# One core, an image filter beside a text encoder: inputs loaded in another order, VectorE's first step in an order of its own, smaller masks, and the residual added inside a feed-forward sum

## The reference

```
h = filter(x)                                  # 8 images of 256 x 256
h = concat([h, text(x_txt)], axis=1)           # 8 sequences of 128 tokens, D = 256
h = h + windowed_attention(layernorm(h))
h = h + spiking_ffn(layernorm(h))              # relu, square, project, count of spikes

filter:  u = sigmoid(2 o);  q = 0
         10 times: q = max(q - 0.5*(d_rows(u)*vf1 + d_cols(u)*vf0), 0)
                   Tq = div_rows(vf1*q) + div_cols(vf0*q);  u = sigmoid(2*(o - Tq))
text:    h = emb[x_txt] + positions
         4 layers: h = ln(h + attention(h));  h = ln(h + relu(h@w1 + b1)@w2 + b2)
```

## Time and profile before

| | |
|---|---|
| time, three runs | median 1001.82 us (1001.42 to 1001.96) |
| the profiled execution's own time | 999.17 us |
| its span, first to last instruction | 997.3 us |
| mean granted TensorE clock | 0.976 |
| busy in the span | PE 905.2, DVE 834.9, ACT 699.3, POOL 122.3 us |

### The profile page before, as it was taken

One profiled execution on the slowest core, in us unless ns is written; L12 is line 12 of the kernel. 1 busy time (PEld: TensorE's weight loads), 2 busy tenths in 40 slices (PEclk: granted clock), 3 DMA queues, 4 the chain that ended last, 5 costly groups with the idle time before them and its releaser, 6 DMA issues.

```text
span 997.3 us, 18874 instructions
## 1 busy us (share of the span) xinstructions
PE 905.2 (91%) x6960; PEld 700.2 (70%) x6960; DVE 834.9 (84%) x1160; ACT 699.3 (70%) x2252; POOL 122.3 (12%) x147
## 2 busy tenths in 40 slices
PE   5489999999999999999999997889998999999997
PEld 4267777777777777777777775767675766667675
DVE  2999999999999999999999998987899599352443
ACT  2666876976877877877876875757767686767842
POOL 6201011011011011101101111101010111000000
PEclk9699999999999999999999999999998999999999
DMA  7311120031010121010220010000001000100000
GB/s 173 113 35 28 66 89 19 22 122 45 18 45 17 32 90 39 17 46 14 70 80 11 17 38 11 12 22 12 27 17 38 17 22 17 44 27 2 17 1 32
DMA packets 24925, 39.00 MB, mean 39 GB/s; under 512 B 4001, under 2 KB 20609, under 8 KB 23553
## 3 DMA queue, kind: packets, MB, share of 16 engines
q1 hardware_dynamic: 24448, 36.74, 11.6%
q0 software_dynamic: 384, 1.05, 0.5%
HBM read 22.21 MB, written 5.24 MB: 28 GB/s over the span
## 4 chain that ended last, share of the span: by engine, by line
DVE 47%; PE 25%; ACT 16%; issue 9%; DMA 2%; POOL 1%; SPq 0%; DVEq 0%; POOLq 0%; ACTq 0%
ACT prob L1086 7%; PE ps_t L849 7%; DVE f L1726 4%; DVE f L1753 4%; PE ps_m L860 4%; DVE f L1748 4%; DVE p L1738 4%; DVE f L1757 4%; DVE neg_max L1762 4%; DVE f L1743 3%; ACT u L1073 3%; DVE f L1721 2%; DVE f L1710 2%; PE ps_s L796 2%; DVE f L1699 2%
## 5 line engine op out<-in xcount | busy, mean ns | idle before, releaser
L1086 ACT ACTIVATE prob<-ps_s,neg_max 128x128 f32<-128x128 f32 x512 | 181.3, 408 | 7.3 <-DVE neg_max L1762 7.3
L1086 ACT ACTIVATION_READ_ACCUMULATOR prob<-ps_s,neg_max 128x1 f32 x512 | 126.6, 249 | 0.0
L655 PE MATMUL ps_t<-w,hidT 128*128 128x256 f32 x512 | 125.7, 383 | 0.0
L1094 ACT ACTIVATE probT<-ps_t 128x512 f32<-128x512 f32 x128 | 81.1, 634 | 44.3 <-PE ps_t L601 28.7
L655 PEld LDWEIGHTS ps_t<-w,hidT 128*128 128x128 f32 x512 | 91.1, 190 | 12.1 <-ACT hidT L1168 3.0
L849 PE MATMUL ps_t<-km,w_fc 128*128 128x384 f32 x256 | 93.9, 503 | 1.0 <-ACT km L1282 1.0
L601 PE MATMUL ps_t<-ident,prob 128*128 128x128 f32 x512 | 81.5, 283 | 12.9 <-ACT prob L1086 6.7
L601 PEld LDWEIGHTS ps_t<-ident,prob 128*128 128x128 f32 x512 | 60.0, 144 | 36.6 <-issue 14.7
L1762 DVE TENSOR_REDUCE neg_max<-ps_s 128x8 f32<-128x1024 f32 x64 | 77.5, 1211 | 4.6 <-PE ps_s L591 4.6
L1341 ACT ACTIVATE prob<-ps_s,neg_max 128x128 f32<-128x128 f32 x192 | 53.8, 376 | 22.6 <-DVE neg_max L1935 22.2
L849 PEld LDWEIGHTS ps_t<-km,w_fc 128*128 128x128 f32 x256 | 47.5, 195 | 26.8 <-issue 3.7
(11 more groups left out here) (179 smaller groups left out, 2038.9 us busy)
## 6 DMA issues: line engine op xcount, KB each, us to landing
w<-in_w SPq DMA_DIRECT2D x8, 1024.0 KB, 5.0
u<-u SPq DMA_DIRECT2D x80, 63.0 KB
p<-p SPq DMA_DIRECT2D x80, 63.0 KB
w_attn<-in_w_attn SPq DMA_DIRECT2D x4, 768.0 KB, 5.4
out<-w SPq DMA_DIRECT2D x7, 384.0 KB, 2.5
o_all<-in_o SPq DMA_DIRECT2D x4, 512.0 KB, 3.7
filtered<-f_out SPq DMA_DIRECT2D x4, 512.0 KB, 3.2
x<-filtered SPq DMA_DIRECT2D x8, 256.0 KB, 2.8
```

The source lines that it names most:

```text
L655: last = mm(ps_t[:, 0, D * t:D * t + D], hidT[:, m, P * t:P * t + P], w2[:, m], start=False, stop=(m == MC - 1), skip_group_check=True)
L1086: last = A(prob[:, n % 2, hh], ps_s[n % 2][:, hh], ACT.Exp, scale=-1.0, bias=neg_max[:, n % 2, hh:hh + 1], accum_out=den)
L1094: A(probT[:, 4 * half:4 * half + 4].rearrange("p h k -> p (h k)"), ps_t[:, 1], ACT.Copy).then_inc(s["act_pT"], 1)
```

## The change

Five things are altered.

1. SyncE issues the first images right behind the tokens, then taps, positions, the four parts of the field (the two for the columns first, with a semaphore of their own each way) and the projection weights last. GpSimd waits for these weights before it issues gathers three to eight.
2. TensorE, VectorE and SyncE start on the first eight constants. The head mask gets its own semaphore, the row masks move behind iteration 0.
3. VectorE's `first_step` has an order of its own: iteration 0's steps before the first `head_max`, and others moved (below).
4. The window masks are 128 x 128, built four times smaller, and read four times over by a stride of zero (PE L788, ACT L1347).
5. The feed-forward bank is opened by the first product with `w2`, which now waits for the third part of the hidden layer, and `carry_ffn` stands later: in a block behind `turn_probs(a, 2, 0)`, in `fuse_first` behind `tile_turn(0, 2, 1)`.

```diff
         @block.sync
             sp.dma_start(tokens[:], d["tokens"]).then_inc(s["l_tok"], 16)
+            load_images(0).then_inc(s["l_img"], 16)
             sp.dma_start(taps[:, 0:18], ...)
             sp.dma_start(taps[:, 18:36], ...)
             sp.dma_start(pe[:], d["pe"]).then_inc(s["l_pe"], 16)
-            load_images(0).then_inc(s["l_img"], 16)
+            for comp, loaded in ((1, "l_vf"), (0, "l_vf_rows")):
+                for img in range(2):
+                    sp.dma_start(vf[64 * img:64 * img + 64, comp], ...).then_inc(s[loaded], 16)
             sp.dma_start(w_attn[:, :, 0:3 * D], ...).then_inc(s["l_qkv"], 16)
-            for img in range(2):
-                for comp in range(2):
-                    sp.dma_start(vf[64 * img:64 * img + 64, comp], ...).then_inc(s["l_vf"], 16)
...
-            sp.wait_ge(s["c_pool"], N_CONST)
+            sp.wait_ge(s["c_pool"], N_EARLY)
             rows_below(0)
...
                 if b == 1:
                     const(pool.memset(v[:], 0.0))
+                    pool.wait_ge(s["l_qkv"], 16)
...
-            def carry(bank, src):
+            def carry(bank, src, first):
-                        mm(..., ident[:], start=(t + c == 0), stop=False, ...)
+                        mm(..., ident[:], start=(first and t + c == 0), stop=False, ...)
             def carry_ffn(k):
                 pe_.wait_ge(s["pool_hr"], k + 1)
-                pe_.wait_ge(s["act_ff1"], 4 * k + 3)
-                carry(ps_t[:, 0], hT_r)
+                carry(ps_t[:, 0], hT_r, False)
...
             def ff2(k, parts):
-                        pe_.wait_ge(s["act_ff1"], 4 * k + part + 1)
+                        pe_.wait_ge(s["act_ff1"], 4 * k + max(part + 1, 3))
-                        last = mm(ps_t[...], hidT[...], w2[:, m], start=False, ...)
+                        last = mm(ps_t[...], hidT[...], w2[:, m], start=(part == 0 and m == 0), ...)
...
-                    m = mask[:, 1].rearrange("p a k -> p (a k)")
+                    m = mask[:, 1].unsqueeze(1).to_broadcast([P, 4, P])
...
             def first_step():                      # VectorE
+                head_pairs()
                 columns_apart(0)
                 columns_weighed(0)
-                head_max(0, 0)
+                positions_first()
                 rows_apart(0)
...
```

More of the change, by code:

```diff
@@ L88, in build @@
         ones = sb("ones", [P, 4 * P])
-        mask = sb("mask", [P, 2, 4, P], BF16)
+        mask = sb("mask", [P, 2, P], BF16)
         head_mask = sb("head_mask", [P, 2])
@@ L546, in carry @@
                         at = D * t + P * c
-                        mm(bank[:, at:at + P], src[:, c, P * t:P * t + P], ident[:], start=(t + c == 0), stop=False, skip_group_check=True)
+                        mm(bank[:, at:at + P], src[:, c, P * t:P * t + P], ident[:], start=(first and t + c == 0), stop=False, skip_group_check=True)
             def carry_attn(k):
@@ L652, in ff2 @@
                     if t == 0:
-                        pe_.wait_ge(s["act_ff1"], 4 * k + part + 1)
+                        pe_.wait_ge(s["act_ff1"], 4 * k + max(part + 1, 3))
                     for m in range(2 * (part % 4), 2 * (part % 4) + 2):
-                        last = mm(ps_t[:, 0, D * t:D * t + D], hidT[:, m, P * t:P * t + P], w2[:, m], start=False, stop=(m == MC - 1), skip_group_check=True)
+                        last = mm(ps_t[:, 0, D * t:D * t + D], hidT[:, m, P * t:P * t + P], w2[:, m], start=(part == 0 and m == 0), stop=(m == MC - 1), skip_group_check=True)
                 if part == 7:
@@ L687, in block_step @@
                 turn_probs(a, 2, 0)
+                carry_ffn(f)
                 ff2(f, range(2, 6))
@@ L1139, in keys_out @@
             def keys_out(k, g):
+                if k == 0:
+                    act.wait_ge(s["c_heads"], 1)
                 act.wait_ge(s[f"pe_k{g}"], k + 1)
@@ L1346, in tile_mask @@
                 for hb in range(2):
-                    last = A(quad[hb], mask[:, 0].rearrange("p a k -> p (a k)"), ACT.Copy)
+                    last = A(quad[hb].rearrange("p (a k) -> p a k", a=4), mask[:, 0].unsqueeze(1).to_broadcast([P, 4, P]), ACT.Copy)
                 last.then_inc(s["f_mask"], 1)
@@ L1669, in _, with head_pairs, row_pairs, positions_first @@
                     dve.sem_inc(s["gen_free"], 1)
[L1671 to L1682 removed]
+            dve.wait_ge(s["c_pool"], N_EARLY)
+            pe_rows = pe[:].unsqueeze(1)
+            def head_pairs():
+                dve.tensor_reduce(head_mask[:], ident[:].rearrange("p (j o d) -> p o j d", o=2, d=TKD), AX.XY, ALU.add).then_inc(s["c_heads"], 1)
+            def row_pairs():
+                for r in range(4):
+                    tick(dve.tensor_reduce(row_mask[:, r:r + 1], ident[:, 32 * r:32 * r + 32], AX.X, ALU.add))
+                dve.wait_ge(s["chain"], chain[0])
+                link(tt(pair_mask[:], row_mask[:, 0:2], row_mask[:, 2:4], ALU.add))
+                ts(pair_mask[:], pair_mask[:], SCALE_F, None, ALU.mult).then_inc(s["c_scaled"], 1)
+                dve.wait_ge(s["c_scaled"], 1)
+            def positions_first():
+                dve.wait_ge(s["g_emb_first"], 32)
+                dve.wait_ge(s["l_pe"], 16)
+                tt(h[:, 0:2], h[:, 0:2], pe_rows.to_broadcast([P, 2, D]), ALU.add).then_inc(s["h_ready"], 1)
             def positions_rest():
@@ L1872, in first_step @@
                 flux_rows(0)
+                flux_cols(0)
+                head_max(0, 0)
+                divergence_columns(0)
                 head_max(0, 1)
-                flux_cols(0)
-                divergence_columns(0)
                 divergence_rows(0)
@@ L1892, in first_step @@
                 divergence_columns(1)
+                normalise(0, 0)
                 divergence_rows(1)
+                normalise(0, 1)
                 divergence_both(1)
                 divergence_out(1)
-                normalise(0, 0)
-                normalise(0, 1)
                 restart()
```

47 lines of the change are left out of this document (19 added, 28 removed).

## The result

The changed kernel takes 1013.94 us (median of 4 runs, 1012.32 to 1014.38) where the kernel before takes 1001.89 in the same comparison: ratio 1.0118, 95% interval 1.0102 to 1.0134. It is slower, as forecast, but by 12.05 us instead of 5.7, and 1013.94 lies above the range given (999.5 to 1010.5). The profiled execution took 1014.38 us, with a span of 1012.6 and a mean granted clock of 0.964; before it was 999.17, 997.3 and 0.976.

A forecast was written before the change was run, and what follows sets the result against it. VectorE was taken to bound blocks 1 to 15, with idle time in block 0. Start +4.7, residual in `fuse_first` +1.0, blocks and masks 0: +5.7, from 1001.82 to 1007.5 us; own range 1004.7 to 1010.2, 8-in-10 range 999.5 to 1010.5.

The forecast's parts named there:

- The rival in which the rows are not held by the weights: Block 0: carried rows served beside the weights, row divergence at 31.6 us, total 1003.2 us; chance 0.16.
- t: Block 0: the time VectorE begins `divergence_rows(0)`, forecast 35.9 us (before 35.52), bounds 33 to 38.5.
- The start: six gathers later: GpSimd, block 0: gathers three to eight held until weights land at 13.5 us; all in at 24.3, against 19.82.
- What waits for the gathers: SyncE, block 0: weights issued from 24.3 us, last weights and carried rows land 11.6 later, at 35.9.
- From t to the end of block 0: VectorE: block 1 starts at t + 28.4, 64.3 us instead of 59.57, +4.7, with `normalise` waiting 3 us.
- The residual in `fuse_first`: TensorE's chain in `fuse_first`: residual products come on top behind the second turn, +1.0 us, bounds 0 and +1.1.
- Masks and blocks: Mask products and blocks 1 to 15: smaller masks cost 0, residual's move in the blocks 0 (-1 to 0).
- 0.70 on slower: Whole kernel: chance 0.70 of slower than before, against 0.20 faster and 0.10 the same.
- a gain at the start: Block 0: weights near 11 us, a gather in 3, text chain sets block 1 at 54.7; 997.9 us; chance 0.18.
- the point of decision: Block 0: the gain at the start decides from a row divergence start below 30.2 us, 5.7 earlier than forecast.

The follow-up runs named there:

- rows first: Changed kernel with SyncE issuing the carried rows of iteration 0 before it waits for the gathers and issues the weights: 1002.67 us, ratio 0.9994.
- start alone: Changed kernel with the residual and the opening of the feed-forward bank back as in the kernel before: 1010.36 us, ratio 1.0088.
- `normalise` last: Changed kernel with the two normalises of block 0 behind all of iteration 1, as in the kernel before: 1010.32 us, ratio 1.0079.
- the residual alone: Kernel before with only the residual moved behind the turns and the feed-forward bank opened by the first product: 1005.69 us, ratio 1.0025.
- both: Changed kernel with the carried rows of iteration 0 issued ahead of the weights and block 0's normalises behind iteration 1: 1000.44 us, ratio 0.9977.
- not held: Changed kernel without GpSimd's wait for the projection weights before the third gather: 1007.00 us, ratio 1.0034.
- the small masks: Kernel before with only the mask made 128x2x128 and read through a stride of zero: 1001.77 us, ratio 0.9987.
- the old places: Changed kernel with carried rows ahead of the weights, block 0's normalises behind iteration 1, residual and bank opening as before: 996.90 us, ratio 0.9945.
- the filling: Changed kernel, carried rows ahead of weights, normalises behind iteration 1, residual in `fuse_first` right behind the first `w2` product: 997.23 us, ratio 0.9954.
- the last kernel: Changed kernel, carried rows ahead of weights, normalises behind iteration 1, residual placed as before, gathers without the wait for projection weights: 995.53 us, ratio 0.9929.

## Why the prediction failed, by its own steps

**The mechanism held; the size did not.** SyncE waits for the gathers, the carried rows wait behind the weights, VectorE waits for the rows, `normalise` waits for the reciprocals, and `fuse_first` pays for the residual. Each was in the trace, and rows first took the second and the third away. The rival in which the rows are not held by the weights is wrong: it gave them some 2.5 us to land, which is right for an empty queue (2.20 in iteration 1 of the kernel before), but behind the weights they took 7.37, from 31.53 to 38.90. They landed with the tail of the weights: `w2` was in at 39.4, half a microsecond behind them, and without the hold at 32.5, with the rows at 33.17. The Trainium skill ("DMA: Bandwidth & Descriptors", Two DMAs through the same engine are not ordered) promises no order there. The traces agree in that either came first, but in none did the rows pass more than this tail.

**The step that failed is "The start: six gathers later".** It put the last landing at 24.3; it was 26.42, 2.1 of the 3.1 us by which t came too late. Four terms, by the trace after:
- the projection weights landed at 14.41, not at 13.5: +0.9
- from there to GpSimd's first gather passed 0.76 us, which the sum left out: +0.8
- the first two of the six held gathers took 1.86 and 1.43 us of issue and not 0.95: +1.4
- the last gather landed 3.59 us behind its issue, not 4.5: -0.9. That it would be shorter than the 5.4 of the earlier trace rows was right; the Trainium skill's fit ("DMA: Bandwidth & Descriptors", Anatomy of one DMA — SWDGE (gpsimd) path) gives 2.3 us for it as an estimate, and the trace has 3.59 with the queue of SyncE silent.

**What waits for the gathers** was forecast at 11.6 us from the first weight's issue to the landed rows; it was 38.90 - 26.44 = 12.5. So t came out as 38.99, 3.1 over the forecast and 0.5 above its bound of 38.5. **From t to the end of block 0** was t + 28.4 and became t + 29.2, with 4.36 us of waiting instead of 3. Block 1 starts at 68.16 instead of 64.3: +3.9. The start as a whole costs +8.6 in the traces and +8.8 in the times, where 4.7 was forecast and 7.3 was the upper bound. (Two other profiles with the old order at the start have block 1 at 61.24 and 61.44, so the 59.57 that all is counted from is an early one; counted from these the cost is near 7.)

The bounds were too narrow for a reason that can be read off: they were put on the end of a load and on a landing, but not on the hand-over and the issue between them, which together made +2.2 of the +3.1. The upper bound also took 5.1 us for the last gather where its own limit was 5.4. The lower end of the whole forecast, +2.9, is not the sum of the lower bounds either: +1.8, -1 and 0 make +0.8.

**The residual in `fuse_first`** was forecast at +1.0 by the trace and is +0.90 in it. In the times it costs more, in four comparisons: 0.0025, 0.0030 (whole change against start alone), 0.0032 and 0.0023 of the time, 2.3 to 3.2 us, each uncertain by some 2 to 3 us. They are not four independent ones, since the last two are counted from the same kernel (rows first and `normalise` last); together they speak for more than 0.9, and don't prove it. The sum of the parts then closes: 8.8 + 2.5 makes 11.3, and 12.05 was measured.

**What stays open** is why it costs more than its microsecond. The granted clock looked like an answer: with the residual behind the turns the profiled executions are at the lower level, between 600 and 700 us, for 20.5, 17.1, 17.1, 17.1, 17.1 and 13.6 us (the changed kernel, the residual alone, rows first, `normalise` last, both, not held); with something in the gap it is 10.2, 10.2, 17.1, 13.7, 13.7 and 17.1 (before, the start alone, the small masks, the old places, the filling, and the last kernel). The means are 17.1 and 13.7. But the profiles speak against the residual in `fuse_first` as the cause. Most of this low time lies ahead of the residual's products; behind them, up to 700 us, it is 3.4 us in eleven of the twelve profiles, wherever the residual stands (6.8 in the residual alone). Nor do the other executions show it: the mean granted clock over all runs of a kernel is 0.969 with the residual moved alone (12 runs) and 0.970 in the kernel before (29 runs); it is 0.968 for rows first and `normalise` last, 0.968 for the same with the residual in its old places, and 0.969 for the same with the filling.

What the low time does cost can be read from the same profiles. From `shift_a` of block 15 to the start of the third tile's scores all kernels do the same work, up to the residual's place in the last block:

| low time from 600 us to the residual's products | profiles | `shift_a` of block 15 to the scores |
|---|---|---|
| 6.8 us | before, the start alone | 60.5 to 60.6 us |
| 10.2 us | the residual alone, not held, the old places, the filling | 61.7 to 61.8 us |
| 13.7 us | rows first, `normalise` last, both, the small masks, the last kernel | 62.3 to 63.0 us |
| 17.1 us | the changed kernel | 64.3 us |

With each 3.4 us more at the lower level the stretch is 0.9 to 1.6 us longer. (Eight of the profiles have another 3.4 us between `shift_a` and 600 us, which is not counted; it may be part of the first step of the table.) The changed kernel's profile has the most low time and that of before the least, and this goes with 3.7 of the 5.5 us that I could not place. Why an execution gets more or less of it is open: the start alone has as little as the kernel before, and the small masks and the last kernel, with the residual in its old places, have as much as three with it moved.

**Masks and blocks** at 0 were right: ratio 0.9987 for the masks, 0.2 us over fifteen blocks in the traces. TensorE's waits in the blocks lost the row; what is left at the top is

```profile
PE ps_y L528 <- ACT h L1130: 22.1, 15, 2.3
```

which was 21.7 before. Part of the 7.9 us that were spared came back as another wait, for ScalarE's copies of `prob`, which was 0.2 us before:

```profile
PE ps_t L603 <- ACT probT L1096: 5.1, 13, 0.4
```

The engine that was spared a wait gained nothing, since VectorE sets the blocks.

**The chances.** 0.70 on slower was the right side. That the kernel got slower says little for the sum, since any t above 31.2 gives it. The 0.18 on a gain at the start asked for weights near 11 us, and they landed at 14.4. By the prediction's own terms even 11 would not have done: 11 + 6.3 + 3 + 11.6 is 31.9, above the 31.2 where nothing changes and the 30.2 that it named as the point of decision. The 348 GB/s that spoke for it are of the slice from 4.5 to 6 us, and the first gather was issued at 4.43, so they are not from before the gathers. But a gain was in the same edits: with the rows ahead of the weights and both `normalise` last it is 0.9977, and 0.9945 with the residual in its old places.

## What to carry to other kernels

When an edit puts a wait into a queue, write down everything that stands behind it in the queue and when the other engines will now want it: here VectorE had the rows ready at 20.5 us and not at 32.1, while their DMA stayed behind the weights, and the whole gain, with more, became one wait. A hold that shows no cost once the rows are ahead cost most of 8.8 us where the small DMAs stood behind the bulk, and moving these two ahead gave all of it back (1.0118 to 0.9994). In a chain of hand-overs bound each link, the issue of the DMAs and the way to the next engine too, and not only the long transfers; and in `fuse_first` work on the chain's engine was free only where it filled the time in which another engine was waited for.

## What the runs showed of the hardware

GpSimd's gathers, 128 rows of 1 KB each, took 0.95 us to issue in most places but more in some, with the same instruction:

```profile
15.17 1.86 POOL L422 DMA_INDIRECT h<-in_emb,tok_idx  x1 [7.09 <-DMA w_attn<-in_w_attn]
17.33 1.43 POOL L422 DMA_INDIRECT h<-in_emb,tok_idx  x1 [0.30 <-issue]
19.06 0.95 POOL L422 DMA_INDIRECT h<-in_emb,tok_idx  x1 [0.30 <-issue]
```

VectorE was busy at 15 to 18 us and the gathers of the earlier trace rows ran while it was idle, but it was busy at 19 us too, and without the hold one gather took 1.94 us at 8.15 beside a VectorE step and 0.95 at 8.13 in the last kernel beside the same one. I leave the reason open.

From one execution to the next the same kernel scatters from 998.6 to 1007.5 us (kernel before, 29 runs), and block 1 starts at 59.57, 61.24 and 61.44 in three profiles with the old order at the start (before, the residual alone, the small masks). A single profile stood up to 5.8 us from its kernel's median (1001.18 and 1007.00 for the gathers not held); differences below that need the times of many runs.
